# Fewer small VectorE operations in the routing stage of a two-expert layer, and x loads that are contiguous in memory

## The reference

```python
xn = (x - mean) / sqrt(var + 1e-5)                    # per token
x1  = ifft(fft(xn) * filt).real                       # a fixed linear map, filt from one scalar of xn
bits = (sigmoid(x1 @ W_el + b_el) > 0.5)              # 24 per token
corrected = golay_correct(bits)                       # 12 check bits fix the rest
s = x1 + corrected @ W_le + b_le
probs = softmax(xn @ router_w.T)                      # 8 experts
vals, idx = top_k(probs, 2); w = vals / (vals.sum(-1) + 1e-6)
g = silu(sum_k (xn @ expert[idx_k] + probs[idx_k]) * w_k)
out = x + s * g
```

## Time and profile before

| What | Value |
|---|---|
| Median of three executions | 1231.86 us |
| Profiled execution, its own time | 1235.18 us |
| Its span | 1233.3 us |
| TensorE (PE) busy | 1131.4 us, 92% |
| VectorE (DVE) busy | 1096.8 us, 89% |
| GpSimd (POOL) busy | 877.7 us, 71% |
| ScalarE (ACT) busy | 512.7 us, 42% |

### The profile page before, as it was taken

How to read it: one execution, slowest core, us unless ns; L and a number is a source line. 1 busy time by engine, 2 the same in 40 slices (tenths; PEclk the granted TensorE clock), 3 DMA queues, 4 the chain that set the end, 5 groups by cost and what they waited for, 6 DMA issues and landing times. The chain is left out here.

```text
span 1233.3 us, 26827 instructions
## 1 busy us (share of the span) xinstructions
PE 1131.4 (92%) x6283; PEld 609.0 (49%) x6284; DVE 1096.8 (89%) x2658; ACT 512.7 (42%) x1151; POOL 877.7 (71%) x857
## 2 busy tenths in 40 slices
PE   5998869725889999999999999999999999999996
PEld 4565545412434455555555555555555555555553
DVE  6899969998877889899989998999999899999985
ACT  4476646664655333333333333333333333333332
POOL 1136655648886588777878887888888788888874
PEclk9999989957999999999999999999999999999999
DMA  8669999403446576666667666666666666666663
GB/s 322 242 212 200 198 149 203 81 23 97 150 144 175 147 172 171 171 174 173 174 166 179 173 173 166 176 174 176 172 169 176 171 175 173 170 178 172 174 167 108
DMA packets 216921, 208.74 MB, mean 169 GB/s; under 512 B 166271, under 2 KB 166271, under 8 KB 212786
## 3 DMA queue, kind: packets, MB, share of 16 engines
q1 hardware_dynamic: 184370, 124.31, 42.8%
q0 software_dynamic: 31360, 79.78, 21.9%
q10 hardware_dynamic: 1152, 4.19, 1.3%
HBM read 123.36 MB, written 47.11 MB: 138 GB/s over the span
## 5 line engine op out<-in xcount | busy, mean ns | idle before, releaser
L1435 PE MATMUL banks<-w_hi,arena 128*128 (+1 forms) x1136 | 432.5, 381 | 6.2 <-DMA arena<-arena 5.9
L1436 PE MATMUL banks<-w_lo,arena 128*128 (+1 forms) x1136 | 432.3, 381 | 0.0
L1437 PE MATMUL banks<-w_hi,arena 128*128 (+1 forms) x1136 | 432.2, 380 | 0.0
L716 ACT ACTIVATE arena<-xbuf,inf 128x512 f16<-128x512 f32 x156 | 112.6, 722 | 532.5 <-DVE xbuf L1225 532.2
L529 POOL DMA_INDIRECT xbuf<-in_L_attn_x,gidx x156 | 189.7, 1216 | 78.9 <-issue 66.2
L531 POOL DMA_INDIRECT inf<-token_info,gidx x156 | 200.2, 1283 | 54.0 <-issue 53.4
L508 POOL DMA_INDIRECT pair_tokens<-tok,slot x112 | 112.6, 1005 | 110.4 <-DVE slot L1058 78.4
L569 POOL TENSOR_TENSOR xbuf<-xbuf 128x512 f32<-128x512 f32 x128 | 162.8, 1272 | 35.8 <-DVE xbuf L1294 28.7
L1435 PEld LDWEIGHTS banks<-w_hi,arena 128*128 128x128 f16 x1136 | 111.4, 98 | 134.3 <-issue 17.1
L1437 PEld LDWEIGHTS banks<-w_hi,arena 128*128 128x128 f16 x1136 | 111.5, 98 | 131.5 <-issue 1.7
L535 POOL DMA_INDIRECT out<-xbuf,sidx x128 | 142.6, 1114 | 40.7 <-issue 40.4
(11 more groups left out here) (305 smaller groups left out, 1728.7 us busy)
## 6 DMA issues: line engine op xcount, KB each, us to landing
xbuf<-in_L_attn_x SPq DMA_DIRECT2D x32, 1024.0 KB, 11.1
arena<-extra_sums SPq DMA_DIRECT2D x128, 256.0 KB
arena<-in_L_ffn_expert_weights SPq DMA_DIRECT2D x8, 1024.0 KB, 11.0
extra_sums<-arena SPq DMA_DIRECT2D x28, 256.0 KB, 2.9
token_info<-info ACTq DMA_DIRECT2D x8, 512.0 KB, 11.5
xbuf<-in_L_attn_x,gidx POOLq DMA_INDIRECT x156
inf<-token_info,gidx POOLq DMA_INDIRECT x156
arena<-arena SPq DMA_TRANSPOSE x128
```

The source lines that it names most:

```text
L716: nc.scalar.activation(hi4[ring(i, k)], uv2[:, b], ACT.Copy, scale=inf2[:, k, 1:2]).then_inc(hi_ready, 1)
L1435: mm(ps, hi[:, c], wh, start=(c == 0), stop=False)
L1436: mm(ps, hi[:, c], wl, start=False, stop=False)
L1437: end = mm(ps, lo[:, c], wh, start=False, stop=(c == C - 1))
```

## The change

- The statistics: the division by 512 and the small constant of the variance go into two operations that take a scalar and two tensors, so that L942 is gone.
- The root: instead of the factor 1.5 - 0.5 r r v the kernel forms (r r v - 3) r, which is -2 times the inverse root, and the factor -0.5 is put into the weights by ScalarE's copies (L631, L634). The operations of L966 and L970 are gone; a row `mean2` in two buffers holds the sum of the means.
- The choice: the differences to the best logit, formed once at the place of the comparison, serve for comparison, second maximum and softmax. L1009 and L1011 are gone.
- The weights: sum and 1e-6 in one operation (L1031 and L1032).
- Token numbers: GpSimd writes them with one iota per round ahead of its scatter, and waits there for the scatter two rounds back; VectorE's L1047, L1057 and L1109 are gone.
- The table rows: the three masks of `tokTf` are built ahead of the marks `in_tile` and `in_lane`, and one multiplication takes the rows as integers. Before, a conversion and three masked operations stood behind the marks.
- Memory: token number = 2048 i + 512 k + 4 p + q in place of 2048 i + 16 p + 4 k + q, for partition p. A load of x is then one run of 1 MB in memory in place of 128 runs of 8 KB that lie 32 KB apart, and a partition's part of the `info` store is four runs of 1 KB in place of one of 4 KB. Tokens get other places in the tiles; their number per pair stays.

```diff
-    x_tiles = x_rows.rearrange("(i p t) e -> p i t e", p=P, t=TB)
+    x_tiles = x_rows.rearrange("(i k p q) e -> p i k q e", p=P, k=U, q=GT)
-    info_tiles = info_dram.rearrange("(i p t) w -> p i t w", p=P, t=TB)
+    info_tiles = info_dram.rearrange("(i k p q) w -> p i k (q w)", p=P, k=U, q=GT)
...
-                sp.dma_start(xbuf[:, k], x_tiles[:, i, k * GT:(k + 1) * GT, :]).then_inc(ld_x[k], 16)
+                sp.dma_start(xbuf[:, k], x_tiles[:, i, k]).then_inc(ld_x[k], 16)
...
-            G.iota(tok[:, 1, :], pattern=[[1, TB]], base=-P * TB - FIRST_TOKEN, channel_multiplier=TB).then_inc(iota_ready, 1)
+            def token_ids(i, buf):
+                G.iota(tok[:, buf, :], pattern=[[P * GT, U], [1, GT]], base=i * P * TB - FIRST_TOKEN,
+                       channel_multiplier=GT).then_inc(iota_ready, 1)
+            token_ids(R - 1, 1)
...
             def scatter(i, buf):
+                after(pool, scattered[buf], 16 * TB * (i // 2))
+                token_ids(i, buf)
+                pool.wait_ge(iota_ready, i + 2)
                 pool.wait_ge(slot_ready, i + 1)
...
-                act.dma_start(info_tiles[:, n], info[:, :, :]).then_inc(info_stored, 16)
+                act.dma_start(info_tiles[:, n], info[:, :, :].rearrange("p (k q) w -> p k (q w)", k=U)).then_inc(info_stored, 16)
...
-                V.tensor_tensor(dev[:, 1], sq_e, sq_o, ALU.add)
-                V.tensor_tensor(dev[:, 2], mean_e, mean_o, ALU.add).then_inc(aggr_ready, 1)
+                V.scalar_tensor_tensor(dev[:, 1], sq_e, E * EPS, sq_o, ALU.add, ALU.add)
+                V.tensor_tensor(mean2[:, i % 2], mean_e, mean_o, ALU.add).then_inc(aggr_ready, 1)
...
-                V.scalar_tensor_tensor(dev[:, 3], dev[:, 0], 0.25, dev[:, 0], ALU.mult, ALU.mult)
-                V.tensor_scalar(dev[:, 1], dev[:, 1], 1.0 / E, EPS, ALU.mult, ALU.add).then_inc(aggr_ready, 1)
+                V.scalar_tensor_tensor(dev[:, 3], dev[:, 0], 0.25, dev[:, 0], ALU.mult, ALU.mult).then_inc(aggr_ready, 1)
...
-                def factor():
-                    dve.wait_ge(newton, 4 * i + 3)
-                    V.tensor_scalar(rt, rt, -0.5, 1.5, ALU.mult, ALU.add).then_inc(newton, 1)
-
                 def final():
-                    dve.wait_ge(newton, 4 * i + 4)
-                    V.tensor_scalar(mean4[:, :], dev[:, 2], 2.0, None, ALU.mult)
-                    V.tensor_tensor(rstd[:, :], r0, rt, ALU.mult).then_inc(rstd_ready, 1)
+                    dve.wait_ge(newton, 3 * i + 3)
+                    V.scalar_tensor_tensor(minus2r[:, :], rt, 3.0, r0, ALU.subtract, ALU.mult).then_inc(rstd_ready, 1)
...
-                lk(V.tensor_tensor(eq, lg, each(m1, NE), ALU.is_equal), beside[1])
+                lk(V.tensor_tensor(dl, lg, each(m1, NE), ALU.subtract), beside[1])
-                lk(V.tensor_tensor(sc, eq, along(ramp_h[:, :], NE), ALU.mult), beside[2])
+                lk(V.scalar_tensor_tensor(sc, dl, 0.0, along(ramp_h[:, :], NE), ALU.is_equal, ALU.mult), beside[2])
...
-                lk(V.scalar_tensor_tensor(l2, oh1, -3e38, lg, ALU.mult, ALU.add), beside[5])
-                V.tensor_tensor(dl, lg, each(m1, NE), ALU.subtract)
-                lk(V.tensor_reduce(m2, over(l2), AXX, ALU.max), beside[6])
-                V.tensor_tensor(d2, m2, m1, ALU.subtract).then_inc(dx_ready, 1)
-                lk(V.tensor_tensor(eq, l2, each(m2, NE), ALU.is_equal), beside[7])
+                lk(V.scalar_tensor_tensor(l2, oh1, -3e38, dl, ALU.mult, ALU.add), beside[5])
+                V.tensor_reduce(d2, over(l2), AXX, ALU.max).then_inc(dx_ready, 1)
+                if beside[6]:
+                    beside[6]()
+                dve.wait_ge(dx_ready, n + 1)
+                lk(V.tensor_tensor(eq, l2, each(d2, NE), ALU.is_equal), beside[7])
...
-                lk(V.tensor_tensor(den, p1, p2, ALU.add), beside[3])
-                lk(V.tensor_scalar(den, den, 1e-6, None, ALU.add), beside[4])
+                lk(V.scalar_tensor_tensor(den, p1, 1e-6, p2, ALU.add, ALU.add), beside[3])
...
-                V.tensor_scalar(tokf[:, :], tokf[:, :], float(P * TB), None, ALU.add)
...
-                V.tensor_copy(tok[:, buf, :], tokf[:, :])
                 V.tensor_copy(slot[:, buf, :], slotf).then_inc(slot_ready, 1)
...
+            V.tensor_scalar(tokTf[:, 1], iota_c, tsel[:, 1, 2:3], None, ALU.is_lt)
             link(V.scalar_tensor_tensor(place_lane, place_tile, -float(P), place_f, ALU.mult, ALU.add))
+            V.tensor_scalar(tokTf[:, 0], iota_c, tend[:, 0:1], None, ALU.is_lt)
+            link(V.scalar_tensor_tensor(tokTf[:, 1], iota_c, tsel[:, 1, 1:2], tokTf[:, 1], ALU.is_ge, ALU.mult))
...
+            dve.wait_ge(rows_loaded, 32)
+            V.tensor_tensor(tokTf[:, :, :], tokT[:, :, :], tokTf[:, :, :], ALU.mult)
             dve.wait_ge(last_mm, 1)
-            V.tensor_copy(tokTl, psum[:, 0, 0:P])
-            dve.wait_ge(rows_loaded, 32)
-            link(V.tensor_copy(tokTf[:, :, :], tokT[:, :, :]))
...
+            V.tensor_copy(tokTl, psum[:, 0, 0:P]).then_inc(rows_float, 1)
```

More of the change, by code:

```diff
@@ L153, in build @@
         dev = sb("dev", [P, 4, TB])
+        mean2 = sb("mean2", [P, 2, TB])
         rt1 = sb("rt1", [P, 4, TB])
-        rstd = sb("rstd", [P, TB])
-        mean4 = sb("mean4", [P, TB])
+        minus2r = sb("minus2r", [P, TB])
         rsc = sb("rsc", [P, 5, NE, TB])
@@ L631, in _ @@
             nc.scalar.activation(msb, psum[:, 2, 0:C * GOLAY_N].rearrange("p (c n) -> p c n", c=C), ACT.Copy,
-                                 scale=1.0 / CS).then_inc(m_copied, 1)
+                                 scale=-0.5 / CS).then_inc(m_copied, 1)
             act.wait_ge(rt_mm, 1)
             nc.scalar.activation(wcat[:, :, 0:NE], psum[:, 4, H:H + C * NE].rearrange("p (c n) -> p c n", c=C),
-                                 ACT.Copy).then_inc(m_copied, 1)
+                                 ACT.Copy, scale=-0.5).then_inc(m_copied, 1)
             norm(1)
@@ L937, in deviations @@
                 V.tensor_tensor(dev[:, 0], mean_e, mean_o, ALU.subtract)
-                V.tensor_tensor(dev[:, 1], sq_e, sq_o, ALU.add)
-                V.tensor_tensor(dev[:, 2], mean_e, mean_o, ALU.add).then_inc(aggr_ready, 1)
+                V.scalar_tensor_tensor(dev[:, 1], sq_e, E * EPS, sq_o, ALU.add, ALU.add)
+                V.tensor_tensor(mean2[:, i % 2], mean_e, mean_o, ALU.add).then_inc(aggr_ready, 1)
                 dve.wait_ge(aggr_ready, 2 * i + 1)
-                V.scalar_tensor_tensor(dev[:, 3], dev[:, 0], 0.25, dev[:, 0], ALU.mult, ALU.mult)
-                V.tensor_scalar(dev[:, 1], dev[:, 1], 1.0 / E, EPS, ALU.mult, ALU.add).then_inc(aggr_ready, 1)
+                V.scalar_tensor_tensor(dev[:, 3], dev[:, 0], 0.25, dev[:, 0], ALU.mult, ALU.mult).then_inc(aggr_ready, 1)
                 dve.wait_ge(aggr_ready, 2 * i + 2)
-                V.tensor_tensor(rt1[:, 0], dev[:, 1], dev[:, 3], ALU.add).then_inc(var_ready, 1)
+                V.scalar_tensor_tensor(rt1[:, 0], dev[:, 1], 1.0 / E, dev[:, 3], ALU.mult, ALU.add).then_inc(var_ready, 1)
             NONE = [None] * (U - 1) * GT
@@ L956, in square @@
                 def square():
-                    dve.wait_ge(newton, 4 * i + 1)
+                    dve.wait_ge(newton, 3 * i + 1)
                     V.tensor_tensor(rt, r0, r0, ALU.mult).then_inc(newton, 1)
                 def product():
-                    dve.wait_ge(newton, 4 * i + 2)
+                    dve.wait_ge(newton, 3 * i + 2)
                     V.tensor_tensor(rt, rt, ve, ALU.mult).then_inc(newton, 1)
-                def factor():
-                    dve.wait_ge(newton, 4 * i + 3)
-                    V.tensor_scalar(rt, rt, -0.5, 1.5, ALU.mult, ALU.add).then_inc(newton, 1)
                 def final():
-                    dve.wait_ge(newton, 4 * i + 4)
-                    V.tensor_scalar(mean4[:, :], dev[:, 2], 2.0, None, ALU.mult)
-                    V.tensor_tensor(rstd[:, :], r0, rt, ALU.mult).then_inc(rstd_ready, 1)
-                return [first, square, product, factor, final]
+                    dve.wait_ge(newton, 3 * i + 3)
+                    V.scalar_tensor_tensor(minus2r[:, :], rt, 3.0, r0, ALU.subtract, ALU.mult).then_inc(rstd_ready, 1)
+                return [first, square, product, final, None]
             def over(a):
@@ L987, in choose @@
             def choose(n, beside=NONE):
-                lk = chain(route_a, 12 * n)
+                lk = chain(route_a, 11 * n)
                 dve.wait_ge(rstd_ready, n + 1)
                 dve.wait_ge(back_done, U * (n + 1))
-                V.tensor_tensor(lat[:, :, :], psum[:, 4, 0:TB * NL].rearrange("p (t n) -> p n t", n=NL), each(rstd[:, :], NL),
+                V.tensor_tensor(lat[:, :, :], psum[:, 4, 0:TB * NL].rearrange("p (t n) -> p n t", n=NL), each(minus2r[:, :], NL),
                                 ALU.mult).then_inc(lat_copied, 1)
@@ L1021, in weigh @@
             def weigh(n, beside=NONE):
-                lk = chain(route_c, 8 * n)
```

(10 more changed lines are left out.)

3 lines of the change are left out of this document (removed).

## The result

The changed kernel takes 1243.61 us (median of seven runs, 1241.24 to 1246.59) against 1231.92 us for the kernel before in the same series (seven runs, 1227.79 to 1237.16). The ratio is 1.0104, 95% interval [1.0081, 1.0127]: slower, and above the predicted range. Its profiled execution took 1243.61 us, span 1241.8 us. VectorE lost 5.9 us of busy time as intended (1090.9 for 1096.8 us) and the end still came later.

What follows compares the result with a forecast made beforehand. Routing was taken as bound by VectorE to 98 us, DMA backlog to 195 us, then TensorE and VectorE; -1.9 + 0 - 0.5 - 0.65 + 0.3 = -2.75 us from 1231.86 gives 1229.1 us, 8-in-10 range 1214 to 1236.

Steps and rivals of the forecast that it cites:

- Rounds 1 and 2: Routing from 72 to 98 us: VectorE sets the pace, so fewer small operations start the DMA backlog earlier, -1.9 us.
- x late from 98 us: Routing rounds 3 to 5, 98 to 195 us: VectorE's 2.4 us gain only lengthens its waits for x, 0.
- waits for x of 12 to 13 us: Sign of the forecast: VectorE's waits for x grow by about 2.4 us; under 8 us speaks for rival 2 or rival 1.
- rival 2: Routing loads: contiguous x frees the DMA queue and the 10.5 us stall goes, -17 us, 1215 us; half-way 1222; chance 20%.
- rival 1: Routing stage: VectorE alone sets the pace, backlog gives way and TensorE follows, -6.5 us, 1225.4 us; chance 15%.
- The end of the sort: Last choice, weights and sort: -0.65 us in all, of which -1.25 from TensorE starting 0.33 us after the copy, not 1.58.
- The stores of info: Info stores in 1 KB pieces: +0.1 us of DMA time each, three counted in the backlog, +0.3 us.
- Rival 3: Info stores in the backlog: each packet costs 0.233 us whatever its size and holds up x, 1245 us; chance 9%.
- a bound of 1.5 us: Last round's wait for the info store of the round before: loss counted as 0.5 us, bounds 0 and 1.5.
- V: Rival theory of the experiments, routing stage: a quicker VectorE loses by itself where x is late, whatever the layout; no chance given.

Runs made afterwards that it cites:

- e3: Changed kernel with info stored in runs of 4 KB as before, x still contiguous: 1220.09 us, 0.9966 of the kernel before.
- e1: Changed kernel with the memory layout of before, keeping the small operations: 1217.75 us, 0.9942 of the kernel before.
- e5: The changed kernel itself, run again on a quick chip beside the kernel before: 1217.17 us, ratio 0.9953.
- e15: The changed kernel once more, on a quick chip (kernel before 1223.21 us): 1219.22 us, ratio 0.9961.
- e18: Changed kernel's small operations with the layout of before, on the chip of e15: 1217.90 us, 0.9954 of the kernel before.
- e17: Changed kernel with two more info stores per round that hold the buffer, as e11, on the chip of e15: 1261.17 us, 1.0315 of the kernel before.
- e11: Changed kernel storing info twice more in each of six rounds, buffer free only when these land; slow chip: 1291.81 us, 0.9907 of the kernel before.
- e13: The changed kernel once more, on a slow chip (kernel before 1303.45 us): 1275.66 us, ratio 0.9806.
- e12: Changed kernel with the same extra stores as e11, from a spare buffer nobody waits for; same chip: 1275.49 us, 0.9780 of the kernel before.

## Why the prediction was wrong

*Rounds 1 and 2, -1.9 us.* Right, if a little small. Scatters start at 77.76, 103.29 and 128.79 us, where the kernel before has 79.78, 105.50 and 131.76: 2.0 us earlier at first, 3.0 us at the third.

*x late from 98 us, the gain lost to it, 0.* The pressure was there (share 0.94 and 0.99), but the sign I looked for, waits for x of 12 to 13 us, did not come: VectorE's is 1.0 us. The waits for the store in these rounds, 7.8 and 14.5 us on ScalarE, give the loads their time. Before the second of them, at 186.52 us, the changed kernel is 8.4 us ahead, more than the forecast's 1.9; how much of that is contiguous x no run isolates, so rival 2 stays open for this chip (on a quick one e3, contiguous, is no faster than e1). On the quick chips, where x arrives in time, rival 1 is about right: it said -6.5 us, and e5, e15, e1 and e18 give -6.7, -4.0, -6.2 and -5.3 us.

*The end of the sort.* The mechanism was right. From the copy of TensorE's sum to its next matmuls I expected 0.33 us; in e15 it is 254.92 - 254.58 = 0.34:

```profile
254.58 0.29 DVE L1160 COPY latT<-banks 128x128 f32<-128x128 f32 x1
...
254.92 1.93 PE L1414 MATMUL banks<-latT 128*128 128x156 f32 x6 [0.38 <-DVE latT L1160]
```

In the recorded run it is 279.59 - 279.25 = 0.34 as well, though the multiplication waited 1.09 us for the table rows ahead of it.

*The stores of info, +0.3 us: the step that failed.* I priced "the stores of info in pieces of 1 KB" by the time that they hold DMA engines, and that price was fair: in 98 to 151 us the store's queue holds the same share before and after, which are:

```profile
q10 hardware_dynamic: 288, 1.05, 8.0%
```

```profile
q10 hardware_dynamic: 998, 1.00, 8.0%
```

(The sums behind it took small packets for large ones: in 74:80 16 of the 155 packets are under 512 B, so one of 8 KB took 0.36 us and not 0.326, and in 66:71 the counts are 127 and 431, so one of 2 KB took about 0.07 us and not 0.085. Nothing hangs on it.) Rival 3 looked at the same object and asked again only what a packet costs others; its 0.233 us per packet did not come (0.057). That its 1245 us lies near the measured 1243.61 us is luck. Neither asked when the store lands and who waits for the buffer. The row was in sight: the earlier trace rows has VectorE waiting 0.49 us for this very store, so the cover was already at zero. I used that row for the last round alone, with a bound of 1.5 us, and priced the waits of the rounds in the backlog at nothing; they came to 24.2 us on ScalarE and 14.3 us on VectorE, all but 2.0 us of them there. And I never followed ScalarE's copies, behind which `latT` and TensorE stand.

The size fits. In the round that lost the time, 14.5 us of ScalarE's wait cost 40.1 - 22.6 = 17.5 us, 1.2 us per us, as in e17. Over the whole stage ScalarE waits 24.2 - 3.3 = 20.9 us more for the store than before, by the prices of e11 and e17 (0.94 and 1.2) some 20 to 25 us; the waits for x, which are nearly gone, give some 10 us back. An estimate of 10 to 15 us is left. The profiled pair differs by 8.4 us, and the gain of 4.0 to 6.7 us that the quick chips show was missed too: 12 to 15 us together. By the medians, 11.7 us apart, it is 16 to 18 us, a little more than the estimate.

The same trace speaks against V: at 186.52 us the changed kernel, with its quicker VectorE and x late, was 8.4 us ahead.

Shown is that a held buffer gives this chain and this loss, that the recorded loss lies in the round with the longest such wait, and that neither operations nor layout lose anything where the store lands in time. Not shown by an experiment is why the store took 25 to 28 us on the recorded chip, how much of that is the runs of 1 KB, and that two buffers or the old layout mend it there: no run fell on such a chip, and the added loads did not imitate it. That x is dearer there (80 to 85 us per MB for 60) and that the landing grew from 16.4 and 18.3 to 25.6 and 28.3 us with four times the packets is what the traces give; the earlier start of the rounds may have a part in it.
The Trainium skill (DMA: Bandwidth & Descriptors, "Queues, rings and completion order") says that a DMA engine takes turns between its queues, some 9 to 17 descriptors at a turn. By that rule, as an estimate from the page's figures, 8 pieces per engine of the old store go in one turn and 32 of the new need two to four, each behind a turn of x; the price of the piece itself stays small. The traces agree in both (equal share, later landing); no run here isolates the turns.

No version beats the changed kernel by more than the intervals. The operations with the old layout (e18, 1217.90 for 1219.22 us; e1) are as quick as any, and their stores in 4 KB runs land a little sooner by the median: 6.3 us in e18, 7.4 us in e15 on the same chip, though the longest there is 12.1 for 9.8 us. So this version gives away nothing on the chips seen. That it would also avoid the loss on the recorded chip is argued and untested.

## What to carry to other kernels

A store has two prices: the time that it holds DMA engines, and the time until its buffer is free. Where a change cuts a store into more pieces, look up its landing, the time to the next write of the buffer, and, in program order, everything that stands behind that write on its engine. A wait of half a microsecond for a store in the trace says that the cover is used up, and that a longer landing is paid in full from there on. And a gain of 0.5% that rests on a DMA queue having room has to be measured on more than one chip.

## What the runs showed of the hardware

- One program differs by chip more than the change does: the kernel before takes 1223 to 1224 us on three chips, 1232 on the recorded one, 1303 to 1305 on two; the changed kernel is 0.5% and 0.4% faster on two, 1% slower on one and 1.9% faster on another. Most of the difference lies in the routing stage: the copy of TensorE's sum at the end of the sort starts at 254.58 us in e15 and at 300.30 us in e13, 45.7 us of the 53.1 between the two spans.
- Engine time for x and expert weights while scatters run beside them: 80 us per MB on the recorded chip, 60 on that of e5. The unit price of a transfer read from one trace holds for that chip.
- With waits spread out in the routing stage the mean granted clock was 0.81 in place of 1.00 (e17 against e15, 98 to 151 us), and a microsecond of ScalarE's waiting cost 1.2 us there.
- In the windows shown a store of 512 KB in pieces of 1 KB cost 30 to 36 us of engine time on the recorded chip, some 2 us of all sixteen, and landed after up to 28.3 us. Its price in engine time does not give its landing.
- Twelve extra stores of 512 KB, 6.3 MB, moved the time by nothing measurable (e12 against e13, within some 9 us) while nobody waited for them.
